# Deeper rings of raw weights, lists read row by partition, and one transfer for each expert's gate and up weights

## The reference, cut to what matters

```python
x = x + xattn(layernorm(x), ctx, mask)        # 16 batches of 112 tokens, width 512
h = layernorm(x)
top_val, top_idx = top_k(softmax(h @ gate_weight.T), 8)      # 64 experts
# some experts are mapped onto similar ones ("rerouted"), then for each expert e:
gate, up = split(h[its tokens] @ gate_up_proj[e].T, 2)       # 192 + 192 columns
y = (silu(gate) * up) @ down_proj[e].T
out = x + sum over a token's 8 experts of weight * y
```

## Time and profile before

| | us |
|---|---|
| median of 3 runs | 804.4 (804.34 to 804.52) |
| the profiled execution | 807.05 |
| its span, first to last instruction | 805.3 |
| TensorE busy in the span | 676.6 (84%) |
| VectorE busy | 541.6 (67%) |
| ScalarE busy | 450.7 (56%) |
| GpSimd busy | 516.2 (64%) |

### The profile page before, as it was taken

The page is one execution under the profiler, slowest core; times in us unless marked ns, Lnnn a source line. Parts: engine busy times, 40 slices in busy tenths (PEclk is TensorE's granted clock), DMA queues, the critical chain, the costliest instruction groups (busy, mean ns, idle before and its releaser), DMA issues. The chain is left out here.

```text
span 805.3 us, 15215 instructions
## 1 busy us (share of the span) xinstructions
PE 676.6 (84%) x4278; PEld 560.5 (70%) x4278; DVE 541.6 (67%) x1213; ACT 450.7 (56%) x891; POOL 516.2 (64%) x461
## 2 busy tenths in 40 slices
PE   4999999630599999999998998999988998989730
PEld 2555565320589999888988888878877977878630
DVE  5699898861276667776677777776767777767611
ACT  3444454310366666666775766757666676666610
POOL 6037777776738877887766666676657666666421
PEclk9999999855599999999999999999999999999965
DMA  8999999505659999999999999999999999999576
GB/s 304 349 313 332 322 330 301 170 12 159 177 154 220 244 240 237 239 247 255 247 268 256 268 241 259 245 245 258 236 260 217 250 236 245 233 246 232 107 132 152
DMA packets 107557, 189.93 MB, mean 236 GB/s; under 512 B 33521, under 2 KB 35441, under 8 KB 106065
## 3 DMA queue, kind: packets, MB, share of 16 engines
q1 hardware_dynamic: 74274, 125.61, 50.2%
q0 software_dynamic: 33200, 63.35, 38.9%
HBM read 143.40 MB, written 56.24 MB: 248 GB/s over the span
## 5 line engine op out<-in xcount | busy, mean ns | idle before, releaser
L1223 PE MATMUL bank<-xh,w1h 128*128 128x256 f32 (+7 forms) x768 | 229.3, 299 | 21.4 <-DVE h L887 21.2
L1224 PE MATMUL bank<-xl,w1h 128*128 128x256 f32 (+7 forms) x768 | 220.5, 287 | 0.0
L1225 PE MATMUL bank<-xh,w1l 128*128 128x256 f32 (+7 forms) x768 | 220.4, 287 | 0.0
L608 POOL DMA_INDIRECT xg<-normed_tokens,list x145 | 159.3, 1099 | 62.5 <-issue 55.9
L1223 PEld LDWEIGHTS bank<-xh,w1h 128*128 128x128 f32 x768 | 147.5, 192 | 27.0 <-issue 26.7
L617 POOL DMA_INDIRECT out_rows<-ys,list x73 | 116.7, 1599 | 72.9 <-ACT ys L1040 60.4
L903 DVE TENSOR_TENSOR xl<-bank,xh 128x448 fp32r<-128x448 f32 (+3 forms) x145 | 84.3, 616 | 115.1 <-ACT xh L1047 115.0
L592 POOL DMA_INDIRECT list_table<-token,slot x112 | 112.4, 1004 | 69.7 <-ACT token L1001 35.9
L617 POOL DMA_INDIRECT second_sum<-ys,list x70 | 111.2, 1589 | 64.5 <-ACT ys L1040 43.5
L1224 PEld LDWEIGHTS bank<-xl,w1h 128*128 128x128 f32 x768 | 147.9, 193 | 0.1
L1225 PEld LDWEIGHTS bank<-xh,w1l 128*128 128x128 f32 x768 | 147.6, 192 | 0.0
(11 more groups left out here) (204 smaller groups left out, 1084.7 us busy)
## 6 DMA issues: line engine op xcount, KB each, us to landing
raw<-in_w SPq DMA_DIRECT2D x195, 256.0 KB, 4.7
raw<-in_w2a SPq DMA_DIRECT2D x65, 256.0 KB, 5.0
ctxT_s<-in_ctxT SPq DMA_DIRECT2D x16, 768.0 KB, 7.3
ctx_s<-in_ctx SPq DMA_DIRECT2D x16, 768.0 KB, 8.8
raw<-in_w2b SPq DMA_DIRECT2D x65, 128.0 KB, 5.9
list_table<-blank SPq DMA_DIRECT2D x30, 256.0 KB, 7.6
x_in<-in_x SPq DMA_DIRECT2D x16, 224.0 KB, 4.5
out_rows<-x SPq DMA_DIRECT2D x16, 224.0 KB, 8.8
```

The source lines that it names most:

```text
L608: pool.indirect_dma_start(xg[u.on(XGS)][0:u.m, t, :], None, normed, bass.IndirectOffsetOnAxis(ap=lists[u.on(LISTS)][0:u.m, t, 0:1], axis=0 ...
L1223: pe.matmul(bank[m][:, 0:W], wh, mh, start=(c == 0), stop=False)
L1224: pe.matmul(bank[m][:, 0:W], wh, ml, start=False, stop=False)
L1225: mm = pe.matmul(bank[m][:, 0:W], wl, mh, start=False, stop=(c == DK - 1))
```

## The change

It does four things. `raw1` becomes a ring of 6 and `raw2` one of 5; the added buffers lie in memory that phase 1 uses for other things. SP issues the weights that many units ahead: the gate and up weights of units 0 to 4 and the down weights of 0 to 3 stand ahead of the wait for the table, those of unit 5 and 4 stand behind the first four lists. A list is read so that partition p holds rows p*nt to p*nt+nt-1, one run of nt x 64 bytes, in place of rows p, m+p, 2m+p, which are nt runs of 64 bytes. The gate and up weights come in one transfer of 6144 bytes a partition.

```diff
-RAW1, LISTS, XGS = 3, 8, 3
-W1_PARTS = 3
+RAW1, RAW2, FRONT, LISTS, XGS = 6, 5, 5, 8, 3
+W1_PARTS = 1
...
+        raw1 += [sb(f"raw1_{i}", [P, DK * 2 * F]) for i in range(3, RAW1)]
+        raw2 += [sb(f"raw2_{i}", [P, 2, D]) for i in range(2, RAW2)]
...
-                rows = table[bass.ds(at, u.rows), :].rearrange("(t p) c -> p t c", p=u.m)
+                rows = table[bass.ds(at, u.rows), :].rearrange("(p t) c -> p t c", p=u.m)
...
             def load_w2(u):
-                split_wait(sp, w2l_s, u.units_freed(2))
+                split_wait(sp, w2l_s, u.units_freed(RAW2))
...
-            load_w1(Unit(2))
-            load_w2(Unit(1))
+            for n in range(2, FRONT):
+                load_w1(Unit(n))
+                load_w2(Unit(n - 1))
             for i in range(4):
                 sp.wait_ge(tabled[i], B // 4 * ENTERS * 16)
             for n in range(4):
                 load_list(Unit(n))
+            for n in range(FRONT, RAW1):
+                load_w1(Unit(n))
+            for n in range(FRONT - 1, RAW2):
+                load_w2(Unit(n))
             for r in range(STATIC):
-                if r + 4 == STATIC:
+                if r + RAW1 == STATIC:
                     sp.wait_ge(c_plan, PLAN)
                 early_stage(load_list, r + 4)
                 if r > 0:
-                    early_stage(load_w1, r + 2)
-                early_stage(load_w2, r + 1) if r > 0 else None
+                    early_stage(load_w1, r + RAW1 - 1)
+                    early_stage(load_w2, r + RAW2 - 1)
```

More of the change, by code:

```diff
@@ L220, in program @@
         prow = sb("prow", [1, 2 * E + 2 * MAX_OVER + 1], I32)
-        raw1 = [sb(f"raw1_{i}", [P, DK * 2 * F]) for i in range(RAW1)]
+        raw1 = [sb(f"raw1_{i}", [P, DK * 2 * F]) for i in range(3)]
         raw2 = two("raw2_", [P, 2, D])
@@ L288, in program @@
         plan_ps = sem("plan_ps"); c_plan = sem("c_plan")
-        w1_in = [sem(f"w1_in{i}") for i in range(RAW1)]; w2_in = sem2("w2_in")
+        w1_in = [sem(f"w1_in{i}") for i in range(RAW1)]; w2_in = sems("w2_in", RAW2)
         list_in = [sem(f"list_in{i}") for i in range(LISTS)]
@@ L487, in load_w2 @@
             def load_w2(u):
-                split_wait(sp, w2l_s, u.units_freed(2))
+                split_wait(sp, w2l_s, u.units_freed(RAW2))
                 e = weights_of(u)
-                sp.dma_start(raw2[u.on(2)][:, 0, :], w2a[bass.ds(e, 1)].rearrange("a p f -> (a p) f")).then_inc(w2_in[u.on(2)], 16)
-                sp.dma_start(raw2[u.on(2)][0:FR, 1, :], w2b[bass.ds(e, 1)].rearrange("a p f -> (a p) f")).then_inc(w2_in[u.on(2)], 16)
+                sp.dma_start(raw2[u.on(RAW2)][:, 0, :], w2a[bass.ds(e, 1)].rearrange("a p f -> (a p) f")).then_inc(w2_in[u.on(RAW2)], 16)
+                sp.dma_start(raw2[u.on(RAW2)][0:FR, 1, :], w2b[bass.ds(e, 1)].rearrange("a p f -> (a p) f")).then_inc(w2_in[u.on(RAW2)], 16)
             load_w1(Unit(0))
@@ L521, in _ @@
             split_wait(sp, w1_in[LAST.on(RAW1)], (overs + LAST.turn(RAW1) + 1) * 16 * W1_PARTS)
-            split_wait(sp, w2_in[LAST.on(2)], (overs + LAST.turn(2) + 1) * 32)
+            split_wait(sp, w2_in[LAST.on(RAW2)], (overs + LAST.turn(RAW2) + 1) * 32)
             split_wait(sp, gathered[LAST.on(XGS)][0], (overs + LAST.turn_of_tile(XGS, 0) + 1) * 16)
@@ L915, in w2_low @@
                 b = u.on(2)
-                v.tensor_tensor(w2l[b][:], raw2[b][:, 0, :], w2h[b][:, 0, :].bitcast(F32), ALU.subtract)
-                v.tensor_tensor(w2h[b][FR:P, 1, :], raw2[b][0:FR, 1, :], w2h[b][0:FR, 1, :].bitcast(F32),
+                v.tensor_tensor(w2l[b][:], raw2[u.on(RAW2)][:, 0, :], w2h[b][:, 0, :].bitcast(F32), ALU.subtract)
+                v.tensor_tensor(w2h[b][FR:P, 1, :], raw2[u.on(RAW2)][0:FR, 1, :], w2h[b][0:FR, 1, :].bitcast(F32),
                                 ALU.subtract).then_inc(w2l_s, 1)
@@ L1054, in w2_high @@
             def w2_high(u):
-                act.wait_ge(w2_in[u.on(2)], (u.turn(2) + 1) * 32)
+                act.wait_ge(w2_in[u.on(RAW2)], (u.turn(RAW2) + 1) * 32)
                 wait(act, y_ps, u.tiles_freed(2))
                 b = u.on(2)
-                a.copy(w2h[b][:, 0, :], raw2[b][:, 0, :])
-                a.copy(w2h[b][0:FR, 1, :], raw2[b][0:FR, 1, :]).then_inc(w2h_s, 1)
+                a.copy(w2h[b][:, 0, :], raw2[u.on(RAW2)][:, 0, :])
+                a.copy(w2h[b][0:FR, 1, :], raw2[u.on(RAW2)][0:FR, 1, :]).then_inc(w2h_s, 1)
             w1_high(Unit(0))
```

## The result

The changed kernel takes 810.8 us (median of 7 runs, 810.18 to 814.19) against 804.5 us before (7 runs, 803.95 to 807.6). The ratio is 1.0081, with a 95% interval of 1.0068 to 1.0094: slower by 0.8%, 5.5 to 7.6 us.

What follows compares the result with a forecast made beforehand. It took TensorE to bound three-tile stages and a ring over ScalarE and VectorE, not DMA, the two-tile ones. Start +0.9 and tail +1.6 us summed to +2.5, from 804.4 to 806.9 us; range 803.8 to 810.0.

Steps and rivals of the forecast that it cites:

- part 1: Deeper weight rings in steady state: 0, as each issue keeps its wait and no engine waits for weights.
- Part 2: Lists by partition: 0, hidden, other end -0.3 us; took 11776 packets under 512 bytes as list rows.
- Part 3: Loads ahead of the first product, before and behind the first lists: +0.9 us, taken as 0.3 and 0.6.
- The second amount: Loads behind the first four lists, 1.18 MB and then unit 6's: 0.6 us, ends 0 and 1.5.
- Part 4: Tail, packets of 6144 bytes beside the merge: +1.6 us, from 2.8 in place of 1.14; ends 0 and +2.4.
- The even turns: In the tail, queues 0 and 1 alternate one packet each, so longer weight packets take more time from the merge.
- Part 5: Long packets in steady state: 0; gathers at most 1.6 us later, taken up by idle time.
- the cover: Two-tile stages: a 2.05 us gather wait left stage length unchanged, and ScalarE still had 1.67 us idle before `hh`.
- Rival B: Two-tile stages: gathers get later by more than the idle time absorbs, much slower, 818 us; chance 0.08.
- Rival C: Queue relieved, gathers stop being late, TensorE's 8.5 us of waits become progress: 795.9 us; chance 0.07.
- A: Nothing to be seen: start and tail terms shrink to 0.5 us or less in sum, 804.9 us; chance 0.26.

Runs made afterwards that it cites:

- late_fill_short: late_fill with gate and up weights again in three parts of 2048 bytes a partition; 805.75 us, ratio 0.9996 to the kernel before.
- before_again: The kernel before, unchanged, run again at the slow time of the chip; 841.4 us, ratio 1.0008.
- lists_alone: The kernel before with only the lists read by partition, at the slow time; 840.0 us, ratio 0.9996.
- packet_alone: The kernel before with only gate and up weights in one transfer of 6144 bytes a partition, at the slow time; 839.3 us, ratio 0.9992.
- rings_alone: The changed kernel with packets and lists as before, keeping rings of 6 and 5 and SP's order, at the slow time; 847.2 us, ratio 1.0091.
- rings_alone2: rings_alone repeated at the usual time; 808.1 us, ratio 1.0035 to the kernel before.
- front_alone: late_fill with FRONT = 5: gate and up weights of units 0 to 4, down 0 to 3, ahead of the first lists; 810.6 us, ratio 1.0074.
- changed_again: The changed kernel, unchanged, for a second trace and time; 810.3 us, ratio 1.0059 to the kernel before.
- merge_alone: The kernel before with fewer weights ahead of the first lists, and in the last loop the next weights waiting for the merge; 804.9 us, ratio 0.9993.
- late_fill: The changed kernel with SP's issues around the start as before, rings filled from stage 5 on; 807.5 us, ratio 1.0030 to the kernel before.

## Why the prediction was wrong in size

**Bound and part 1, right.** The two-tile stages have the length of before, there is no wait for weights to remove, and late_fill_short shows full rings at 0.9996.

**Part 2, right:** nothing measurable by itself. But its row was misread: the 11776 small packets are not all list rows. From 500 to 740 us before_again has 12156 of them and lists_alone, with half the list packets, 9082, which is a quarter fewer and not half; packet_alone, with two transfers fewer a unit, has 936 fewer, about 16 for each transfer saved. The estimate didn't use the 11776.

**Part 3, mis-sized, and this is the step that failed.** Taken as 0.3 + 0.6 us, measured as 1.7 to 2.6 and 1.5. Its working had the weights "end near 199, and the first list is issued at 198.94", and read that as a tie that costs next to nothing. But SP issues the list when the last rows of the table have landed, and those rows were written beside the weights: DMA share 1.03 from 190 to 195 us where it was 0.28. All but 0.12 MB of the weights were through by 196, 3 us ahead of the working's 199, and the list was late all the same. The wait moved, and the list with it. The text treated 198.94 as a fixed time and not as the end of a transfer. It also took SP's own issues for free. In the changed kernel's two traces they do end in time, at 190.0 and 191.4; where phase 1 ends early against the weights they alone put the list 13.3 us behind the last entry (rings_alone). The second amount was bounded rightly by 1.5 us and taken at 0.6, on the argument that most would have drained; the whole bound was the measurement. The row's length has a part in it: with short packets the same loads made 0.56 us (rings_alone2, 16.20 against 15.64), with long ones 1.3 to 1.5 (the two traces of the changed kernel against front_alone).

**Part 4, right in its mechanism, over-sized.** +1.6 was taken. At the usual time the merge took 23.5 to 24.0 us in the six traces with long packets and 22.7 to 23.1 in the five with short ones, about 0.9 more; beside 840 us it was 23.80 against 22.4 to 22.7. The even turns held (162 to 158; 163 to 160 in the same stretch of changed_again's merge). Against the 21.29 us of merge_alone, the one trace without weights beside the merge, short packets cost it 1.4 to 1.8 us and long ones 2.2 to 2.7, where the working had 1.14 and 2.8: what it under-priced most is what the merge had paid before. The 3.0 us a MB were too dear for long packets: 1.93 us for 0.74 MB is 2.6. The Trainium skill, as weighed there (DMA: Bandwidth & Descriptors, Queues, rings and completion order), has turns by whole packets, which agrees. That a turn's length wouldn't hang on the row's length was the prediction's own inference from it, and is not borne out, since the merge got longer.

**Part 5, right.** Gathers got later, with a median of 6.8 us from issue to landing where it was 6.3, TensorE's waits for them went from 8.5 to 15.0 us, and the cover held. Rival B did not come about. Rival C neither, and A is out.

The direction came out, but not by the sum as it stood: of its 2.5 us 1.6 lay in the tail, and of the 4.0 to 4.9 us in the two traces four fifths lie at the start.

**Left open.** The first trace of the changed kernel explains 4.0 of 6.5 us, the second all of the 4.8 us measured beside it, that of late_fill 0.7 of 2.4, and that of front_alone, which is of a run 3.4 us faster than its median, 1.8 of 6.0. The runs of front_alone spread over 6 us. That in its slower runs SP's issues come late, as in rings_alone at 840 us, fits, but no trace of such a run at the usual time shows it. A version with FRONT at 4 wasn't tried.

## What to carry to other kernels

Before deepening a ring, look whether anybody waits for what it holds; if not, there is nothing to gain, and what its filling costs hangs on when it is done: 0.35% around the first lists, nothing measurable from stage 5 on. Loads issued "while nothing else is going on" at a phase's end share the DMA engines with the last writes that the next phase waits for, and an in-order queue puts the urgent small transfer behind all of them: put the small lists first, and hold the bulk until the first gathers have landed (-0.2% to -0.3% here). That gain came by way of the gathers: with the weights of three units ahead the list already followed the last entry by 1.97 us, and with those of two it still did. A time at which a transfer is issued is not a fixed point in a prediction if it follows another transfer's landing.

## What the runs showed of the hardware that was not expected

The same kernel took 840.6 us at one time and 804.9 us at another, with stages of 8.24 us in both. In the traces 31.8 of the 32.2 us between the spans lie ahead of the first product (246.41 against 214.58). The DMA engines don't look like what held it up: from 60 to 120 us they and TensorE were both less busy than at the usual time. Columns as in rows 2, before, then before_again:

```profile
60.00:120.00 60.00, 58.33 (x273) 35.19 (x271) 53.62 (x228) 28.89 (x86) 46.05 (x46) 0.97 0.97 329
```

```profile
60.00:120.00 60.00, 50.46 (x216) 27.44 (x214) 43.99 (x186) 21.94 (x71) 35.63 (x38) 0.97 0.80 266
```

In each of the four traces of that time ScalarE waits 10 to 12 times, at most 3.8 to 5.1 us each, ahead of the same step (L1000, in rings_alone L1007) for something that the profile only calls remote; the twelve traces at the usual time have no such wait between 40 and 200 us. In before_again, 40 to 160 us:

```profile
ACT slot L1000 <- remote: 36.5, 10, 3.8
```

What it waited for is open. A time of the one beside a time of the other says nothing; the ratios to the kernel before at the same time, +0.91% and +0.35% for rings_alone and rings_alone2, still agree in sign.
